# A four-layer graph network: the rows carried across quarters summed by TensorE instead of three broadcast rows on VectorE

## The reference

```
x = _layernorm(x + _L0_gnn_ref(...))
x = _layernorm(x + _L1_gnn_ref(x, edge_attr_2, L1_gnn_weight, edge_index))
x = _layernorm(x + _L2_gnn_ref(...))
x = _layernorm(x + _L3_gnn_ref(...))

# in L1: a message of 32 numbers per edge, then
out = jax.ops.segment_sum(msg, edge_index[0], num_segments=n_nodes)
```

## Time and profile before

| | |
|---|---|
| median of 3 runs | 17495.23 us (17494.18 to 17500.92) |
| the profiled execution, its own time | 17499.07 us |
| its span, first to last instruction | 17497.3 us |
| mean granted TensorE clock | 0.729 |
| DVE busy | 12714.1 us, 73% of the span |
| POOL busy | 12574.8 us, 72% |
| PE busy | 6372.7 us, 36% |
| ACT busy | 3721.7 us, 21% |

### The profile page before, as it was taken

How to read it: one execution, slowest core, us unless ns; L and a number is a source line. 1 busy time by engine, 2 the same in 40 slices (tenths; PEclk the granted TensorE clock), 3 DMA queues, 4 the chain that set the end, 5 groups by cost and what they waited for, 6 DMA issues and landing times. The chain is left out here.

```text
span 17497.3 us, 146366 instructions
## 1 busy us (share of the span) xinstructions
PE 6372.7 (36%) x33457; PEld 4980.7 (28%) x33457; DVE 12714.1 (73%) x18056; ACT 3721.7 (21%) x6097; POOL 12574.8 (72%) x13055
## 2 busy tenths in 40 slices
PE   1111111110444444444320000000006888888885
PEld 0000000000333333333320000000005777777774
DVE  7777777774899999999663333333337999999996
ACT  1000000000222222222751111111112222222221
POOL 7777777777677777777127777777777777777775
PEclk9999655555777777777665555555558999999997
DMA  6333333331111111111332222222222222222221
GB/s 162 97 97 95 97 99 97 97 95 45 29 28 28 28 28 27 27 28 24 145 122 59 59 59 59 59 59 59 59 52 47 53 55 54 53 55 54 53 56 35
DMA packets 801746, 1107.09 MB, mean 63 GB/s; under 512 B 422003, under 2 KB 564265, under 8 KB 788794
## 3 DMA queue, kind: packets, MB, share of 16 engines
q0 software_dynamic: 422176, 503.42, 13.1%
q1 hardware_dynamic: 303551, 402.93, 8.3%
q10 hardware_dynamic: 75736, 197.70, 3.0%
HBM read 715.27 MB, written 389.49 MB: 63 GB/s over the span
## 5 line engine op out<-in xcount | busy, mean ns | idle before, releaser
L1872 POOL DMA_INDIRECT s_arena<-d_t,s_arena x6250 | 5902.9, 944 | 2015.3 <-issue 1901.2
L1844 POOL DMA_INDIRECT s_arena<-d_t,s_arena x3125 | 3065.9, 981 | 1019.1 <-issue 933.0
L1821 POOL DMA_INDIRECT d_pay<-s_arena x3125 | 3026.8, 969 | 992.3 <-issue 934.7
L1580 PE MATMUL psall<-s_arena 128*128 128x500 bf16 x1875 | 870.5, 492 | 4252.1 <-DVE s_arena L583 3842.8
L1493 ACT ACTIVATE s_arena<-s_arena 128x800 f32<-128x800 f32 x250 | 429.1, 1716 | 6161.2 <-DVE s_arena L1163 6161.2
L1684 PE MATMUL psall<-s_w2r,s_arena 128*128 128x384 f32 x4750 | 1708.1, 493 | 7.5 <-DVE s_arena L1027 6.6
L960 DVE TENSOR_TENSOR s_arena<-s_arena,psall 128x2400 f32<-128x2400 f32 x125 | 332.0, 2656 | 1739.5 <-DMA s_arena<-d_t,s_arena 1739.5
L1580 PEld LDWEIGHTS psall<-s_arena 128*128 128x128 bf16 x1875 | 198.8, 106 | 4825.1 <-DVE s_arena L583 4263.0
L1684 PEld LDWEIGHTS psall<-s_w2r,s_arena 128*128 128x128 f32 x4750 | 1430.7, 315 | 87.6 <-DVE s_arena L1027 18.7
L1770 PE MATMUL psall<-s_tails,s_mfix 128*128 128x32 f32 x6 | 1.9, 412 | 3972.0 <-DVE s_tails L1171 3972.0
L1036 DVE TENSOR_REDUCE s_arena<-s_arena 128x64 f32<-128x1024 f32 x1000 | 1397.4, 1408 | 0.0
(11 more groups left out here) (289 smaller groups left out, 17064.9 us busy)
## 6 DMA issues: line engine op xcount, KB each, us to landing
s_arena<-d_t,s_arena POOLq DMA_INDIRECT x9375, 2.5
d_scan<-s_arena ACTq DMA_DIRECT2D x375, 400.0 KB, 2.5
s_arena<-d_ew SPq DMA_DIRECT2D x126, 800.0 KB
s_arena<-d_pay SPq DMA_DIRECT2D x33, 1650.0 KB, 6.8
d_inj<-s_agg SPq DMA_DIRECT2D x125, 400.0 KB, 4.0
s_arena<-d_inj SPq DMA_DIRECT2D x125, 400.0 KB, 3.4
d_pay<-s_arena POOLq DMA_INDIRECT x3125
d_pay<-s_agg SPq DMA_DIRECT2D x100, 429.0 KB, 3.0
```

Source lines behind the costliest of these rows:

```text
L1580: e.matmul(R5s[:, 0:4], lhsT, rhs[:, 0:4], start=start, stop=True, skip_group_check=True)
L1821: e.indirect_dma_start(pay_d, bass.IndirectOffsetOnAxis(ap=S1.adr[s4][:, t:t + 1], axis=0), S1.pay[s4][:, 33 * t:33 * t + 33], None).then_ ...
L1844: e.indirect_dma_start(L3.gb[s][:, t], None, T3_d, bass.IndirectOffsetOnAxis(ap=L3.idx[s][:, t:t + 1], axis=0)).then_inc(sem(f"g3_{s}"), 16)
L1872: e.indirect_dma_start(L.gb[s][:, t * L.CW:(t + 1) * L.CW], None, L.tab, bass.IndirectOffsetOnAxis(ap=L.idx[s][:, t:t + 1], axis=0)).then_ ...
```

## The change

Three edits.

1. SP reads the three last rows once, into three partitions (`F1.tail` is now 3 x 3200), instead of three times 125 partitions.
2. TensorE turns `cross` (125 x 3) into 3 x 125, VectorE copies that from PSUM into `F1.crossT`, and TensorE multiplies: seven matmuls with 3 rows of weights, 125 columns out, over 3200 columns, into PSUM from column 512 on. VectorE adds that once to `agg`. TensorE then waits for that addition, since the table behind it uses the same PSUM banks.
3. The small read d0i is issued right behind x, and TensorE's first wait covers both (`ld_x` up to 32); its own semaphore and SP's wait on it are gone.

```diff
-        F1.tail = [cv(NJ * 32) for _ in range(3)]
+        F1.tail = cv(NJ * 32)[0:3]
+        F1.crossT = cv(NP)[0:3]
...
                 e.memset(agg[0:NP, :], 0.0).then_inc(dv.up(), 1)
                 mk[layer, "frow"] = dv.n
+                e.wait_ge(sem("pe_left"), 1)
+                e.tensor_copy(F1.crossT, ps[0][0:3, 0:NP]).then_inc(dv.up(), 1)
+                mk["crossT"] = dv.n
             after(e)
             if layer == 1:
                 e.wait_ge(sem("ng1"), 16 * 32)
 
-                for r in range(3):
-                    e.wait_ge(sem("ld_tail"), 16 * 3)
-                    after(e)
-                    e.scalar_tensor_tensor(out=agg[0:NP, :], in0=F1.tail[r][0:NP], scalar=cross[0:NP, r:r + 1], in1=agg[0:NP, :], op0=ALU.mult, op1=ALU.add).then_inc(dv.up(), 1)
+
+                e.wait_ge(sem("pe_left"), 2)
+                e.tensor_tensor(agg[0:NP, :], agg[0:NP, :], psall[0:NP, 512:512 + NJ * 32], ALU.add).then_inc(dv.up(), 1)
+                mk["left"] = dv.n
...
-                e.wait_ge(sem("ld_x"), 16)
+                e.wait_ge(sem("ld_x"), 32)
...
+            if layer == 1:
+
+                e.transpose(ps[0][0:3, 0:NP], cross[0:NP, 0:3], ident[0:NP, 0:NP]).then_inc(sem("pe_left"), 1)
+                e.wait_ge(sem("ld_tail"), 16)
+                e.wait_ge(dv.h, mk["crossT"])
+                for o in range(0, NJ * 32, 512):
+                    w = min(512, NJ * 32 - o)
+                    m = e.matmul(psall[0:NP, 512 + o:512 + o + w], F1.crossT, F1.tail[:, o:o + w], start=True, stop=True)
+                m.then_inc(sem("pe_left"), 1)
+                e.wait_ge(dv.h, mk["left"])
...
             e.dma_start(xs[0:NP, :], x_v).then_inc(sem("ld_x"), 16)
+            e.dma_start(d0i[:, :], dst_v[:, 0:1]).then_inc(sem("ld_x"), 16)
...
-            e.dma_start(d0i[:, :], dst_v[:, 0:1]).then_inc(sem("ld_d0i"), 16)
...
-                for r in range(3):
-                    e.dma_start(F1.tail[r][0:NP].rearrange("p (f n) -> p f n", f=32),
-                                fold_d.rearrange("(g f t) n -> g f t n", g=4, f=32)[r:r + 1, :, Q1 - 1].to_broadcast([NP, 32, NJ])).then_inc(sem("ld_tail"), 16)
-                e.wait_ge(sem("ld_tail"), 16 * 3)
+                e.dma_start(F1.tail.rearrange("p (f n) -> p f n", f=32),
+                            fold_d.rearrange("(g f t) n -> g f t n", g=4, f=32)[0:3, :, Q1 - 1]).then_inc(sem("ld_tail"), 16)
+                e.wait_ge(sem("ld_tail"), 16)
...
-            e.wait_ge(sem("ld_d0i"), 16)
```

## The result

| | before | changed |
|---|---|---|
| median, us (6 runs each) | 17496.19 | 17584.3 |
| lowest and highest, us | 17493.82, 17500.92 | 17575.93, 17595.28 |
| profiled execution, us | 17499.07 | 17575.93 |

The ratio is 1.0052 with an interval of [1.0042, 1.0062]: the changed kernel is 88 us **slower**, where 20.7 us less was forecast.

What follows compares the result with a forecast made beforehand. The piece was taken as a wait for the broadcast reads, then VectorE's chain. 13.4 us (wait) plus 7.35 (passes) gave 20.7 less: 17495.23 to 17474.5 us, range 17466 to 17486.

Steps and rivals of the forecast that it cites:

- The piece: Between the barrier and the addition to x: shorter wait wins 13.4 us, one pass for three wins 7.35 us.
- The setup: Moving d0i's read ahead of the W0 and dst reads: -0.8 to +0.8 us, taken as 0.
- The step that failed: From the addition to x up to the next loop: each microsecond won ahead of 9020.97 is won at the end.
- the last of the prediction's own signs of being wrong: At the program's end: prediction is wrong if the addition to x moves as said and the end doesn't.
- The rival that came true: Long loops change pace for an unseen reason, either way, a few us to some 40; chance 6%.
- the rows did not go one after the other: Rival, new read: each partition's 32 rows go in turn, 2.3 us each, giving 17514.5 us; chance 2%.
- the gathers did not need as long: Rival, wait before the addition: gathers need as long as the reads did, only passes won, 17487.9 us; chance 3%.
- the setup did not slip: Rival, setup: d0i's four-byte rows delay dst and the search, up to +15 us, 17475 to 17490; chance 5%.

Runs made afterwards that it cites:

- the four steps: Changed kernel plus four idle semaphore steps on VectorE ahead of layer 3's loop: 17494.32 us, 0.9987 of the kernel before (17518.47 us beside it).
- two reductions a round: Changed kernel with four idle VectorE steps, plus two unused reductions atop each of layer 3's 30 rounds: 17592.85 us, 1.004 of the kernel before.
- both loops held: Changed kernel with 35 idle VectorE steps ahead of the spread's loop, none ahead of layer 3: 17497.04 us, 0.9986 of the kernel before.

## Why the prediction was wrong

*The piece: right.* 20.9 us measured for 20.7 forecast: pass 3.49 us (3.51 forecast), the wait ended by the gathers, matmuls in 11.02 us (14.1 forecast at 2.4 GHz and 28.2 at 1.2; the clock was at 0.50 throughout, so the price taken from the earlier trace rows was some 2.5 times too high, and nothing hung on it). VectorE's pass started 8992.09 - 8944.48 = 47.6 us behind SP's read, where the forecast had 8996.7 - 8949.0 = 47.7.

*The setup: a sign missed.* The forecast had the first loop's start within 0.8 us of 189.46; it came at 184.91, 4.55 us earlier. Whether the moved read does that is not shown. The seven runs with the read at its old place, the kernel before among them, start that loop between 183.44 and 190.05 us, the eleven with it moved between 183.64 and 186.67. So 189.46 was itself one of the late ones, and scatter alone can give the 4.5 us.

*The step that failed* is the sentence "Everything behind it up to the next loop hangs on that chain and on the barrier at its end, so each microsecond won ahead of 9020.97 should be won at the end". It costed what lies behind the next loop at nothing. The change also took four instructions out of VectorE's stream ahead of layer 3, and that had a price: **102.1 us in layer 3, a term that the sum did not have.** It is the last of the prediction's own signs of being wrong: the addition to x moved as said, and the end of the program didn't. 102.1 less the 25.4 won ahead of it gives the 77 us between the profiled executions; the medians stand 88 apart.

*The rival that came true* was the last, "the long loops change their pace for a reason that I can't see", with 6% and "a few us to some 40". Its size was short by more than half, and its reason was to be seen in the trace of before, in rows that the prediction did not read: the spread's loop idles at its top 30 times with no releaser, and 162 of the 195 instruction packets travel there.

```profile
DVE s_arena L714 <- issue: 92.9, 30, 3.4
...
```

```profile
q14 instruction: 162, 1.33, 0.1%
```

Nothing hung on it there, so it stood far down each list. But it says that a loop of VectorE can be too long for what is kept, and layer 3's 281 instructions began at most two places behind the border: held at 1891, fetched again at 1888.

*The other rivals* fell: the rows did not go one after the other (the matmuls started 3.9 us behind SP's read), the gathers did not need as long (VectorE started 13.5 us earlier, counted from SP's first DMA), the setup did not slip.

*Scatter ahead of the piece.* The runs with the four steps and with two reductions a round, on the same chip, have the same code up to layer 3, and start the first of the 32 gathers behind the fold at 8949.49 and 8967.16 us. Against that, the 4.5 us say nothing of the change.

## What to carry to other kernels

Before costing an edit at nothing, count how many instructions it adds or takes on each engine ahead of a loop, and look whether the instruction queue has packets in that loop, and the engine a wait "issue" once a round: a loop of a few hundred instructions may sit a step from a border. Where it does, a few idle steps ahead of the loop are worth more than the edit (here 4 steps, 100 us), and they pay only where that engine sets the pace. A gap in the engine that feeds TensorE costs more than its length, with TensorE's matmuls late and at the lower clock behind it: here 2.4 us of gap cost 3.2.

## What was not expected of the hardware

- The starts tried, of loops of 281 and 364 instructions, all fit blocks of 128 instructions with three kept. Two blocks of 256, which the page of the Trainium skill named above states, would have held the loops that begin at 2003 and at 714, and these were fetched. The size of the packets fits 128 too: with both loops held, 45 packets of 8.2 KB travel on q14 in the whole run, and the built program has 5635 instructions on VectorE, ScalarE, POOL and SP together, 125 a packet (that q14 is the queue of these four is inferred). A second instruction queue, q8, has packets of 16.4 KB (88 in the kernel before); whose they are the trace doesn't say. The idle time at the top of a round is 2.7 to 3.1 us in the mean (79.0 / 29 in the changed kernel, 92.9 / 30 in the spread).
- Behind gaps of 4.67 to 5.35 us in layer 3 TensorE's next six matmuls were slow in 29 of 29 cases, 4.23 us in place of 2.33 in the one shown, with the clock at 0.51. Behind gaps of 2.53 us at most it was so in 70 of 124 cases of the kernel before: one gap of that length tells nothing.
- Two chips of the three used for experiments ran all of these kernels in 22.7 ms and not 17.5. On them the changed kernel is not slower than the kernel before (0.9984 to 0.9992). Why these chips are slower was not settled.
